# One graph layer: 15 tiles a batch instead of 16, held marks used three times, and another order of VectorE's step

## The reference

```python
msg = jax.nn.relu(node_inputs[src] + edge_inputs)
agg = jax.ops.segment_sum(msg, dst, num_segments=12500)
h = (1.0 + eps[0]) * node_inputs + agg
x = _layernorm(x + (h @ W.T + b), axis=-1)
```

## Time and profile before

| | us |
|---|---|
| time, median of 3 executions | 3082.23 (3078.57 to 3084.59) |
| span of the profiled execution | 2071.9 |
| PE busy in the span | 2016.0 |
| PE weight loads busy | 1922.5 |
| VectorE busy | 1648.3 |
| ScalarE busy | 1565.9 |
| GpSimd busy | 1519.9 |

### The profile page before, as it was taken

How to read it: one execution, slowest core, us unless ns; L and a number is a source line. 1 busy time by engine, 2 the same in 40 slices (tenths; PEclk the granted TensorE clock), 3 DMA queues, 4 the chain that set the end, 5 groups by cost and what they waited for, 6 DMA issues and landing times. The chain is left out here.

```text
span 2071.9 us, 117127 instructions
## 1 busy us (share of the span) xinstructions
PE 2016.0 (97%) x46449; PEld 1922.5 (93%) x46449; DVE 1648.3 (80%) x4231; ACT 1565.9 (76%) x1616; POOL 1519.9 (73%) x1571
## 2 busy tenths in 40 slices
PE   4899999999999999999999999999999999999997
PEld 3899999999999999999999999999999999999994
DVE  7888778888888778888888877888888887788875
ACT  5777777777777777777777777777777777777773
POOL 6577777777777777777777777777777777777770
PEclk9999999999999999999999999999999999999998
DMA  6344454444444444544444444444444444444441
GB/s 163 84 111 113 113 114 114 112 110 109 110 111 112 112 113 114 114 110 110 110 110 110 114 112 113 112 114 109 110 110 110 111 113 113 111 114 114 110 110 34
DMA packets 236283, 228.68 MB, mean 110 GB/s; under 512 B 104218, under 2 KB 185556, under 8 KB 236062
## 3 DMA queue, kind: packets, MB, share of 16 engines
q1 hardware_dynamic: 186177, 202.59, 33.4%
q0 software_dynamic: 50080, 25.74, 13.3%
HBM read 225.43 MB, written 2.71 MB: 110 GB/s over the span
## 5 line engine op out<-in xcount | busy, mean ns | idle before, releaser
L541 POOL DMA_INDIRECT rows_all<-in_x,index x1565 | 1519.4, 971 | 502.8 <-issue 476.5
L1173 PE MATMUL found<-table,oh 128*128 128x128 bf16 x18720 | 1241.3, 225 | 11.5 <-issue 2.5
L1173 PEld LDWEIGHTS found<-table,oh 128*128 128x128 bf16 x18720 | 1168.1, 144 | 43.6 <-issue 20.0
L1012 ACT ACTIVATE oh<-keys,minus_lanes 128x1024 bf16<-128x1024 f16 x195 | 224.2, 1150 | 307.3 <-PE found L1173 294.5
L1154 PE MATMUL l<-xparts,oh 128*57 128x96 bf16 x18720 | 436.2, 207 | 0.9 <-ACT oh L1000 0.9
L1154 PEld LDWEIGHTS l<-xparts,oh 128*57 128x57 bf16 x18720 | 409.4, 108 | 14.0 <-issue 1.1
L993 ACT ACTIVATE oh<-slots,minus_lanes 128x1824 bf16<-128x1824 f16 x195 | 351.3, 1801 | 7.1 <-DMA slots<-slot_dram 7.1
L786 DVE COPY_PREDICATED rows_all<-mask,found 128x256 f32<-128x256 uint16 x780 | 343.1, 440 | 7.6 <-issue 1.4
L968 ACT CAST table<-l 128x768 bf16<-128x768 f32 x390 | 310.9, 798 | 39.7 <-PE l L1154 24.7
L1000 ACT ACTIVATE oh<-oh 128x1824 bf16<-128x1824 bf16 x195 | 335.7, 1721 | 0.0
L780 DVE TENSOR_TENSOR mask<-iota,side 128x32 f16<-128x32 f16 x195 | 37.5, 192 | 303.1 <-PE found L1173 291.0
(11 more groups left out here) (126 smaller groups left out, 906.5 us busy)
## 6 DMA issues: line engine op xcount, KB each, us to landing
slots<-slot_dram SPq DMA_DIRECT2D x195, 456.0 KB
msg<-in_edge SPq DMA_DIRECT2D x390, 128.0 KB
keys<-key_dram SPq DMA_DIRECT2D x195, 256.0 KB
rows_all<-in_x,index POOLq DMA_INDIRECT x1565
index<-in_src SPq DMA_DIRECT2D x195, 4.0 KB
key_dram<-key SPq DMA_DIRECT2D x195, 2.0 KB
slot_dram<-slot_row SPq DMA_DIRECT2D x195, 3.6 KB
oh<-in_x SPq DMA_DIRECT2D x3, 512.0 KB, 6.2
```

What stands on the lines that cost most here:

```text
L541: pool.indirect_dma_start(to, None, x, bass.IndirectOffsetOnAxis(indices[:, j:j + 1], 0)).then_inc(done, 16)
L1012: nc.scalar.activation(key_marks(b), by_edge(keys[:, four, :]), ACT.Square, bias=minus_lanes[:, b:b + 1]).then_inc(keys_squared, 1)
L1173: last = nc.tensor.matmul(found[:, t * FOUND:(t + 1) * FOUND], key_marks(b)[:, :, t], table[:, b, n * FOUND:(n + 1) * FOUND],  start=(b == ...
```

## The change

- POOLED goes from 8 to 7. A batch is 15 tiles, 7 gathered and 8 looked up; there are 208 full batches instead of 195. GpSimd's turns are 3, 2 and 2 gathers.
- In `look_in_table` the marks are loaded as weights for the first of the three table parts only; the other two matmuls are issued as instructions that keep the weights (`stream_again`).
- `sum_tiles` goes through the tiles of both spans in turn instead of one span after the other.
- VectorE's step: the four picks stand back to back right after the early key marks, each waiting for the one before; `add_rows` moves ahead of `find_rank`; the mask moves from before the picks to after `mark_batch`; `add_window` moves to the end of the step and handles the window of the same step's `sum_batch` (one step sooner); the two reads of `base_row` move from the start of the step to between the last key mark and the slot marks. Each pick has a semaphore increment ahead of it (`picks_started`) that nothing waits for.

```diff
-    POOLED = 8
+    POOLED = 7
...
-    TURNS = [(0, 3), (3, 6), (6, POOLED)]
+    TURNS = [(0, 3), (3, 5), (5, POOLED)]
...
             def step(st):
-                first, second = window_base(st, 0), window_base(st, 1)
                 for b in range(EARLY_KEYS):
                     mark_keys(st, b)
-                mark_sides(st)
-                pick(st, 0)
-                after_pick(st, 0)
-                add_window(st, 0, first)
-                pick(st, 1)
-                after_pick(st, 1)
-                add_window(st, 1, second)
-                pick(st, 2)
-                after_pick(st, 2)
+                for k in range(SIDE):
+                    pick(st, k)
                 count_before(st)
-                pick(st, 3)
                 place_sources(st)
+                add_rows(st)
                 find_rank(st)
-                add_rows(st)
                 give_key(st)
                 mark_buckets(st)
                 give_slots(st)
                 pair_buckets(st)
                 for b in range(EARLY_KEYS, DVE_KEYS):
                     mark_keys(st, b)
+                first, second = window_base(st, 0), window_base(st, 1)
                 for j in range(DVE_SUBS):
                     mark_slots(st, j)
                 mark_batch(st)
+                mark_sides(st)
+                add_window(st, 0, first)
+                add_window(st, 1, second)
...
+            def stream_again(to, held, moving, begin, end):
+
+                return nc.tensor.add_instruction(mybir.InstMatmult(
+                    name=nc.get_next_instruction_name(), engine=mybir.EngineType.PE, ldweights=False,
...
-                            last = nc.tensor.matmul(
-                                found[:, t * FOUND:(t + 1) * FOUND], key_marks(b)[:, :, t],
-                                table[:, b, n * FOUND:(n + 1) * FOUND],
...
+                            if n == 0:
+                                last = nc.tensor.matmul(to, key_marks(b)[:, :, t], part, start=begin, stop=end, skip_group_check=True)
+                            else:
+                                last = stream_again(to, key_marks(b)[:, :, t], part, begin, end)
...
             def sum_tiles(n):
-                for g, tiles in enumerate(spans_of(n)):
-                    for j in tiles:
-                        last = nc.tensor.matmul(win_sums(g), relus[:, j, :], onehots[:, j, :], start=(j == tiles.start), stop=(j == tiles.stop - 1))
+                groups = spans_of(n)
+                for j in range(max(len(tiles) for tiles in groups)):
+                    for g, tiles in enumerate(groups):
+                        if j < len(tiles):
+                            last = nc.tensor.matmul(win_sums(g), relus[:, tiles[j], :], onehots[:, tiles[j], :], start=(j == 0), stop=(j == len(tiles) - 1))
                 return last
```

More of the change, by code:

```diff
@@ L429, in take_nodes, with nodes_of_tile @@
             eng.wait_ge(nodes_turned, k + 1)
-            copy(rel[:, 2 * k:2 * k + 2, 0:ROWS], turned_nodes(k)[:, :, 0:ROWS]).then_inc(nodes_taken[k % 2], 1)
+            n = min(2, TILES - 2 * k)
+            copy(rel[:, 2 * k:2 * k + n, 0:ROWS], turned_nodes(k)[:, 0:n, 0:ROWS]).then_inc(nodes_taken[k % 2], 1)
+        def nodes_of_tile(h, rows, j):
+            if j < POOLED:
+                return rel_rows[0:rows, h, 0:P * POOLED].rearrange("b (p t) -> b t p", t=POOLED)[:, j, :]
+            return rel_rows[0:rows, h, P * POOLED:BATCH].rearrange("b (p t) -> b t p", t=LOOK)[:, j - POOLED, :]
         def one(ap3, b):
@@ L677, in take_all_nodes @@
             def take_all_nodes():
-                for k in range(0, TILES // 2, 2):
+                for k in range(0, PAIRS, 2):
                     take_nodes(nc.vector.tensor_copy, dve, k)
@@ L798, in add_rows @@
                     got = slice(0, (SHORT if isinstance(m, int) and m == 0 else TILES) * D)
-                    after_pick(st, SIDE - 1)
+                    if has(st, -1, ROWS):
+                        dve.wait_ge(picked_ready, st.s * SIDE)
                     dve.wait_ge(rows_gathered[slot], gathered(slot, use))
@@ L815, in window_base @@
             def window_base(st, g):
-                if has(st, -2, BATCHES) and not (isinstance(st.s, int) and st.s - 2 < g):
-                    return dve.value_load(base_row[0:1, g, bass.ds(row_of(st.s - 2), 1)], min_val=0, max_val=NODES - 1)
+                if has(st, -1, BATCHES) and not (isinstance(st.s, int) and st.s - 1 < g):
+                    return dve.value_load(base_row[0:1, g, bass.ds(row_of(st.s - 1), 1)], min_val=0, max_val=NODES - 1)
             def add_window(st, g, base):
-                if has(st, -2, BATCHES) and not (isinstance(st.s, int) and st.s - 2 < g):
-                    m = st.s - 2
+                if has(st, -1, BATCHES) and not (isinstance(st.s, int) and st.s - 1 < g):
+                    m = st.s - 1
                     if g == 0:
@@ L1021, in step @@
                 if not st.inside and st.s == 0:
-                    for k in range(1, TILES // 2, 2):
+                    for k in range(1, PAIRS, 2):
                         take_nodes(nc.scalar.copy, act, k)
@@ L1108, in turn_nodes @@
                 pe.wait_ge(late_taken, 1)
-                for k in range(TILES // 2):
+                for k in range(PAIRS):
                     if k >= 2:
                         pe.wait_ge(nodes_taken[k % 2], k // 2)
-                    for t in range(2):
-                        j = 2 * k + t
-                        at = j if j < POOLED else j - POOLED
+                    for j in range(2 * k, min(2 * k + 2, TILES)):
                         for h, b0, b1 in HALF_ROWS:
-                            span = rel_rows[0:b1 - b0, h, :].rearrange("b (g p t) -> b g t p", g=SPANS, t=LOOK)[:, j // POOLED, at, :]
-                            last = nc.tensor.matmul(turned_nodes(k)[:, t, b0:b1], span, ident_half[0:b1 - b0, 0:b1 - b0], start=True, stop=True)
+                            last = nc.tensor.matmul(turned_nodes(k)[:, j % 2, b0:b1], nodes_of_tile(h, b1 - b0, j), ident_half[0:b1 - b0, 0:b1 - b0], start=True, stop=True)
                     last.then_inc(nodes_turned, 1)
@@ L1140, in place_kept @@
                                      xparts[0:KEPT, SUBS * EVEN + b, :, :], start=True, stop=True)
+            def stream_again(to, held, moving, begin, end):
+                return nc.tensor.add_instruction(mybir.InstMatmult(
+                    name=nc.get_next_instruction_name(), engine=mybir.EngineType.PE, ldweights=False,
+                    ins=[nc.tensor.lower_ap(moving), nc.tensor.lower_ap(held, for_matmul_weights=True)], outs=[nc.tensor.lower_ap(to)],
+                    start_tensor_calc=begin, stop_tensor_calc=end, is_transpose=False, tile_size=(P, P), tile_position=(0, 0),
+                    bass_skip_group_check=True))
             def look_in_buckets(st):
```

23 lines of the change are left out of this document (13 added, 10 removed).

## The result

| | before | changed |
|---|---|---|
| time, median of 4 executions | 3083.41 us (3078.57 to 3085.87) | 2928.32 us (2923.95 to 2932.46) |
| span of the profiled execution | 2071.9 (without pauses) | 2929.0 |

The account below looks back on a forecast made before the run. TensorE was taken as the bound at 10.15 us a step, VectorE after the change at 9.45 (break-even 9.515). 208 x 9.45 against 195 x 10.15 gave 13 us less: 3069 us from 3082, range 3030 to 3135.

Parts of the forecast that it names:

- these 1010 us: Median run time above the profiled span: taken as fixed time outside the span, left unchanged by the change.
- the fourth rival: TensorE's instruction stream paces unprofiled runs, 15.3 us a batch: 3254 us priced by matmuls, 2824 with loads; chance 0.09.
- the term of the prediction: TensorE's window sums, alternating between array halves: 0.35 us saved a step, bounds 0.25 and 0.40.
- TensorE's 9.40: TensorE's step: 10.15 us less 0.35 for lookup loads, 0.35 for window sums and 0.05 for the wait for picks.
- (a): VectorE's four picks back to back, 0.10 us between each: chain changes by -0.67 us.
- (b): VectorE's pick to `counts` to `placed`, latency no longer covered by picks: +0.61 us.
- (c): VectorE's `msg` ahead of the reduction, so `key` waits on the reduction's latency: +0.18 us.
- (e): VectorE's window adds at the end of the step, 0.11 us each: +0.22 us.
- (f): The two `base_row` reads on VectorE, ahead of the slot marks: engine stands still +0.65 us, bounds 0 and 0.80.
- the second rival: VectorE's new order costs more, by a longer read hold and later pick starts: 9.69 us a step, 3119 us; chance 0.17.
- The first rival: The `base_row` reads do not hold up VectorE; TensorE's 9.40 us sets the period: 3058 us; chance 0.16.
- the third: TensorE's lookup does not speed up without weight loads: 9.75 us a step, 3131 us; chance 0.16.

Follow-up runs that it names:

- sums_only: Kernel before with only the window sums alternating between the two column groups: 2986.77 us (0.9675) and 2987.03 us (0.9675), both on chips with pauses.
- reloaded: Changed kernel with a weight load for each of the 96 lookups again: 2843.89 us (0.9385) with pauses, 2169.71 us (1.0467) without.
- mixed_reloaded: Changed kernel with all 96 loads, base_row reads after mark_batch, counts between third and fourth pick, reduction before messages: 0.9370 with pauses, 1.0062 without.
- sixteen_reloaded: Changed kernel with 16 tiles (8 gathered), 195 batches and all 96 lookup loads: 2999.78 us (0.9716) on a chip with pauses.
- held_only: Kernel before with only one weight load for three table parts: 3042.97 us (1.0055) with pauses, 2110.61 us (1.0177) without.
- mixed: Changed kernel with base_row reads after mark_batch, counts between third and fourth pick, reduction before messages: 2917.04 us (0.9627) with pauses, 2030.42 us (0.9772) without.

## Why the prediction was wrong

**The step that failed** is the one that the whole sum stands on: "I take these 1010 us as fixed, since no row shows them, and make the sum against the span". The 1010 us were no time outside the span but 5.2 us in each of 195 steps: 4.7 us of pauses and 0.5 us more of everything else. The view that would have raised doubt was at hand: a profile whose span is two thirds of the median does not show the executions that are timed, and its rows bound nothing in them. My reason against the fourth rival, that a step of 15.3 us would leave every engine idle, was no reason: before on a chip with pauses has VectorE at 54%, ScalarE and GpSimd at 50%, and TensorE at 78%. That the sign came out right is luck: the 13 us of the forecast were summed for a chip without pauses, and on such a chip the change loses.

**The fourth rival** had the place right (a step of 15.3 us, paced by TensorE's stream) and the price wrong. By the matmul it gave 3254 us, by matmuls and loads 2824; neither holds, since `sums_only` takes 3.3% off with the same instructions, and `reloaded` is faster than the changed kernel with more of them (0.9385 against 0.9492, on two chips).

**Which parts gave the 5.1%** (chips with pauses, one part added to the other):

- *Alternating sums*: 0.9675 alone, twice. 100 us in 195 steps are 0.52 us a step; the term of the prediction was 0.35, and 30 records within 0.57 us on a chip without pauses make it 0.45.
- *Order of VectorE's step*: 0.9716 with it against 0.9675 without. The intervals overlap; it gave nothing that these runs can tell.
- *15 tiles*: 0.9716 to 0.9385, across two chips. More steps, but 1.7 us shorter ones, with 4.6 pauses instead of 5.7. On one chip `mixed_reloaded`, which has 15 tiles and all loads and another order of VectorE's step, took 2892.8 us beside the 2999.78 of `sixteen_reloaded`, with a step 1.45 us shorter and 4.4 pauses instead of 5.7. I had counted the tiles only as 13 more steps to pay for, and the kernel with the pauses shows them as the second half of the gain.
- *Held marks*: 0.9385 to 0.9492, a loss of 1.1%, across two chips; alone on the kernel before, on one chip, a loss of 0.55%. What falls is the mean granted clock. `held_only` has this edit alone and was at 0.896 beside 0.957 to 0.965 for before; over all kernels on chips with pauses, those with held marks were at 0.896 to 0.909 and those with all loads at 0.941 to 0.975. So the edit lowers the clock where there are pauses; how it does is not shown. That the lower clock is what costs the time is argued: the rest of the step grows from 9.96 to 10.30 us in the first pair, but hardly from `mixed_reloaded` to `mixed` (10.37 and 10.39, on two chips).

**On a chip without pauses**, where the sum was made, its mechanism held and its size did not. VectorE did take over, the hole by the two reads came, the held marks are worth 0.29 us a step and the sums 0.45 (0.35 each in the sum), so TensorE's 9.40 was about right. VectorE's chain was 9.94 us, not 9.45. In the step shown above the terms came out: (a) picks 0.26 more than taken, (b) 0.02 more, (c) 0.09 more, (e) 0.21 more, (f) 0.09 less, together 0.49. The common reason is the start of an instruction that waits for its direct predecessor's end. Over the whole loop a pick starts 0.15 us after the pick before it (median of 447; the 0.26 in the step above is rare), where I took 0.10 between two readings of the earlier trace rows, 0.04 and 0.13; `placed` starts 0.20 us after `counts`, where I took 0.18; `key` 0.20 us after the reduction, where I took 0.13. The window adds had been read at 0.11 each from places with a pick behind them; one behind the other they start 0.21 us apart. The break-even was 9.515 us, and so the second rival (a costlier VectorE, 3119) was the right one for that kind of chip. Of its two reasons the longer start of the picks came, the longer hold did not, and at 4.4% the loss was larger than its price. I had also named TensorE alone as the bound before, though by my own reading the gathers filled the same step; the 15 tiles are what makes room for a shorter one. The first rival (reads that don't hold up the engine) fell with the hole, the third (no gain from fewer loads) with `mixed` against `mixed_reloaded`.

**What stays open** is what the pauses are. They are TensorE's own: the waits are released by issue, and neither a matmul, nor a weight load, nor an instruction of its sequencer starts in them. They are tied to places in the step and not to the jump, and no packets of instructions come with them. In every trace with pauses, 67% to 87% of them have the last matmul before them start while GpSimd executes a gather, which is 50% to 53% of the time; by the end of that matmul it is 52% to 67%. Most pauses, 66% to 93%, fall into the bucket matmuls, and of those 69% to 99% begin during a gather, though only 35% to 48% of all bucket matmuls do. That would fit 15 tiles, with seven gathers a step instead of eight, having fewer. But both the pauses and the gathers stand at fixed places of the step, no run moves one against the other, and on chips without pauses the kernel before executes gathers for 76% of the time and has not one pause. No gain of `sums_only` on a chip without pauses was measured, as both its runs met pauses.

## What to carry to other kernels

Before a sum is made against a profile, hold its span against the timed executions; where they differ by more than their spread, the profile shows another condition than the timed one, and the forecast needs the step of the timed one (here 15.4 us, not 10.15) before any term of it counts. A change should be tried in both: this one gained 5.1% in one and lost 4.4% in the other, and `mixed` gained in both (0.977 and 0.963). With pauses, alternating the two halves in the sums is the simple part and worth 3.3% alone; it was never measured without them. And where an instruction on VectorE waits for its direct predecessor, it started 0.15 us (picks) to 0.20 us (`placed`, `key`) after that one's end in the changed kernel; with another instruction between them, as in before and in `mixed`, nothing of this is seen.

## What the runs showed of the hardware that was not expected

- The same kernel took 2073 to 2078 us on three chips and 3028 to 3091 us on three others, with each chip steady within 0.4%. On the slower ones TensorE stops for about 0.7 us, 4 to 7 times in a step of 427 to 495 instructions, its sequencer's included.
- After such pauses the granted clock was 0.50 for 2.7 us in one step, and its mean was 0.909 over the kernel, though TensorE was never idle for more than half a microsecond at a time there.
- Leaving out two of three loads of the lookup lowered the mean granted clock on a chip with pauses, from between 0.957 and 0.965 down to 0.896. On a chip without pauses it did not change (0.993 in `before` and in `held_only`).
- A loop body of two steps (some 990 instructions) is not brought in again each round (19 instruction packets), one of four steps is (483 packets, +15%).
- 32 small fp32 matmul records that write one half of the array after another take 33 ns each, 30 in turn between the halves 19.5 ns.
